# A decoder in two layers: VectorE takes a row's router logits ahead of the first maximum of an iteration of cross attention

## What is computed

```
x = x + L0_attn(layernorm(x));   x = x + L0_xattn(layernorm(x), ctx);   x = x + L0_ffn(layernorm(x))
x = x + L1_attn(layernorm(x));   x = x + L1_xattn(layernorm(x), ctx);   x = x + L1_ffn(layernorm(x))

xattn:  q, k, v in 16 heads of 16 channels;  scores = q k^T / 4;  softmax over 375 keys;  (attn v) Wo + bo
ffn:    logits = x Wr + br  (8 experts);  the best two (layer 0) or one (layer 1) of 8 experts per token
```

## Time and profile before

| | |
|---|---|
| median of the runs | 1463.95 us (1462.85 to 1476.16) |
| span of the profiled execution | 1473.2 us |
| iterations 3 to 13 of cross attention, layer 0 and layer 1, in that execution | 194.7 us each |
| TensorE busy, matmuls / weight loads | 89% / 70% of the span |
| VectorE, ScalarE, GpSimd busy | 48%, 38%, 30% |

### The profile page before, as it was taken

How to read it: one execution, slowest core, us unless ns; L and a number is a source line. 1 busy time by engine, 2 the same in 40 slices (tenths; PEclk the granted TensorE clock), 3 DMA queues, 4 the chain that set the end, 5 groups by cost and what they waited for, 6 DMA issues and landing times. The chain is left out here.

```text
span 1473.2 us, 34595 instructions
## 1 busy us (share of the span) xinstructions
PE 1305.0 (89%) x13568; PEld 1036.2 (70%) x13568; DVE 701.9 (48%) x1744; ACT 558.2 (38%) x1246; POOL 444.8 (30%) x654
## 2 busy tenths in 40 slices
PE   5998899999998389999994999799999998559996
PEld 2665457777776279999993777557777776459996
DVE  4885345555552612222222999545565552323322
ACT  2776035555554012222221555135555553112221
POOL 5994300000000155556552221200000000135662
PEclk8999579999998589999997999799999997569999
DMA  7000111111110369999984000011111110279994
GB/s 241 2 2 2 23 26 36 36 36 37 36 36 17 128 225 340 346 347 337 329 320 107 1 1 1 15 29 42 44 44 43 42 43 25 80 192 347 356 368 147
DMA packets 61355, 177.89 MB, mean 121 GB/s; under 512 B 20608, under 2 KB 41953, under 8 KB 46756
## 3 DMA queue, kind: packets, MB, share of 16 engines
q0 software_dynamic: 22176, 141.55, 27.0%
q1 hardware_dynamic: 39044, 34.46, 9.2%
HBM read 147.62 MB, written 12.85 MB: 109 GB/s over the span
## 5 line engine op out<-in xcount | busy, mean ns | idle before, releaser
L975 DVE TENSOR_REDUCE xa_mx<-xa_ps_s 112x2 f32<-112x750 f32 x246 | 231.5, 941 | 219.4 <-PE xa_ps_s L704 215.9
L892 ACT ACTIVATE xa_p<-xa_ps_p 125x672 f32<-125x672 f32 x256 | 187.2, 731 | 236.2 <-PE xa_ps_p L710 236.2
L710 PEld LDWEIGHTS xa_ps_p<-xa_qT,xa_kT 32*125 32x125 f32 x3072 | 199.4, 191 | 95.3 <-ACT xa_p L892 66.8
L710 PE MATMUL xa_ps_p<-xa_qT,xa_kT 32*125 32x112 f32 x3072 | 243.4, 291 | 24.4 <-DVE xa_mx L975 10.4
L704 PE MATMUL xa_ps_s<-xa_kT,xa_qT 32*112 32x375 f32 x984 | 224.8, 534 | 1.0 <-DMA xa_qT<-xa_qU 1.0
L1803 PEld LDWEIGHTS ex_ps_h<-ex_xT,ew_w 128*128 128x128 f32 x1792 | 213.7, 196 | 4.8 <-issue 2.0
L1803 PE MATMUL ex_ps_h<-ex_xT,ew_w 128*128 128x128 f32 x1792 | 214.3, 279 | 1.3 <-ACT ex_xT L1833 1.3
L1814 PE MATMUL ex_ps_y<-ew_w,ex_hT 128*128 128x256 f32 x896 | 202.7, 379 | 0.0
L1814 PEld LDWEIGHTS ex_ps_y<-ew_w,ex_hT 128*128 128x128 f32 x896 | 165.9, 190 | 20.2
L1837 ACT ACTIVATE ex_hT<-ex_ps_h,ew_w 128x128 f32<-128x128 f32 x224 | 70.1, 364 | 282.5 <-PE ex_ps_h L1803 282.5
L1849 DVE TENSOR_SCALAR ex_hT<-ex_ps_h,ew_w 128x128 f32<-128x128 f32 x224 | 68.2, 346 | 163.7 <-PE ex_ps_h L1803 163.7
(11 more groups left out here) (304 smaller groups left out, 2000.0 us busy)
## 6 DMA issues: line engine op xcount, KB each, us to landing
xa_kT<-xa_kU SPq DMA_DIRECT2D x128, 93.8 KB, 2.2
xa_qT<-xa_qU SPq DMA_DIRECT2D x64, 56.0 KB
xn<-xa_x SPq DMA_DIRECT2D x32, 112.0 KB, 2.2
lin_yg<-ys SPq DMA_DIRECT2D x16, 224.0 KB, 5.2
cT<-in_ctxT SPq DMA_DIRECT2D x4, 750.0 KB, 8.3
xa_qT<-xa_nmT SPq DMA_DIRECT2D x128, 1.8 KB
x<-in_x SPq DMA_DIRECT2D x4, 448.0 KB, 6.2
xn<-x SPq DMA_DIRECT2D x16, 112.0 KB, 2.1
```

Source lines behind the costliest of these rows:

```text
L710: return pe.matmul(bp[0:CT, i, c * S:(c + 1) * S], kT[r:r + 32, b % RB, n, c * CT:(c + 1) * CT], qT[r:r + 32, b % RB, n, :], start=True, s ...
L892: act.activation(p[slot % 4][:, :, :], bp[0:CT, :, 0:NC3 * S], ACT.Exp).then_inc(exped, 1)
L975: dve.tensor_reduce(mx[:, b % 2, j:j + 2, n], score_banks(b, pair)[0:S, :, 0:CL], AX, ALU.max).then_inc(maxed, 1)
```

## The change

At slot 0 of each iteration, VectorE's list has `row_logits(t-3)` ahead of `maximum`, and not behind it. Nothing else is edited.

```
             for t in range(-3, NB + 3):
                 for slot in range(8):
                     sb, sp = ahead(t, slot)
+                    if slot == 0 and on(t - 3):
+                        row_logits(t - 3)
                     if on(sb):
                         maximum(sb, sp)
-                    if slot == 0 and on(t - 3):
-                        row_logits(t - 3)
                     if slot == 0 and on(t - 2):
                         finish(t - 2)
```

## The result

The changed kernel takes 1453.32 us, the median of 20 runs (1442.10 to 1468.35), against 1462.59 us for the kernel before (20 runs, 1454.66 to 1481.75). The ratio is 0.9928, with a 95% interval from 0.9902 to 0.9953: 0.7% faster, 9.3 us by the medians; the interval is 7 to 14 us. Forecast were 1452.3 us and a gain of 11.7 us.

What follows compares the result with a forecast made beforehand. TensorE, busy for 89% of the span, was taken to bound the kernel. Ending 22 waits at 0.53 us each took 11.7 us off the runs' 1463.95 us, giving 1452.3 us, range 1448.0 to 1462.5 us.

Steps and rivals of the forecast that it cites:

- The wait and its size: Key products, iterations 3 to 13, both layers: they no longer wait for the maximum, 22 x 0.53 = 11.7 us gained.
- VectorE at no cost: Slot 0 on VectorE: row_logits ahead of the maximum delays nothing, costed at nothing.
- its fallback price: VectorE at slot 0, without idle time to hide the moved instruction: at most 0.156 us each, 22 x 0.156 = 3.4 us.
- a sign of being wrong: Prediction wrong if the maximum of round 0 starts later than 0.94 us behind round 0.
- the cover: VectorE's 1.41 us of idle time ahead of the maximum, of which the moved instruction needs 0.156 us.
- the rival's rule: Logits block VectorE: a late router product delays maximum and round 1, 22 us per us beyond 0.49 us; chance 0.01.
- What is late next: Round 1, at 2.37 us behind round 0: maximum, exponential and keys are ready 0.49, 0.60 and 0.9 us ahead.
- None takes the place of the wait: Ahead of round 1, neither maximum, exponential nor key transfers become a new wait.
- The rival that I gave 0.06: Keys land late and round 1 waits: 0.65 us per case, 1460 us if all took 3.3 us; chance 0.06.
- the likeliest case: Full gain in iterations 3 to 13 of both layers, by itself 1448.5 to 1455 us; chance 0.72.
- The span and the median: End of cross attention, layer 1: its 9.7 us clock loss explains the profiled span's 9.25 us above the median.
- The rivals on the clock: Clock falls at cross attention's end: one layer in the median run, 1462.0 us, chance 0.13; both layers, 1471.7 us, 0.04.

Runs made afterwards that it cites:

- the late product: The changed kernel with the router product moved behind the values of the next iteration: 1475.84 us, ratio 1.0031 to the kernel before.

## Why the prediction was right, and where its steps were not

**The wait and its size: right.** 0.53 us an iteration, in place of 0.50 by the idle time, held in 20 of the 22 iterations of the profile, and in all 22 once the keys come in time. Iteration 2 of layer 1 served as a run of the change in the trace before: same work, without the wait. The Trainium skill's sentence on weight loads pulled ahead ("TensorE: Matmul & The Clock Gate", on engine queues) bears on the 0.03 us between the two figures; the trace after agrees: the keys' weights load from 1007.95, while the values' matmuls run to 1008.02, behind 0.18 us of PEld idle time and not 0.72.

**VectorE at no cost: right, its fallback price untested.** The maximum starts 0.95 us behind round 0, a hundredth past the 0.94 that was named as a sign of being wrong, and nothing hangs on it. For the case that the cover were gone I put "at most 0.156 us for each". That can hold only where the product is there in time: in the late product the maximum is put back by 1.27 us, since it waits for as long as the instruction ahead of it does. The Trainium skill states VectorE's strict order ("TensorE: Matmul & The Clock Gate", on the array's architecture); the trace of that run agrees, with 2.29 us of idle time and the scores ready. What such a delay costs an iteration, by the rival's rule 22 us in all for each us beyond the slack of 0.49, stays open, because the keys' wait, and not the maximum, set round 1 there.

**What is late next: wrong in part.** "None takes the place of the wait" is refuted for the keys' transfers, in 2 of 22 iterations, by 1.00 and 0.73 us. The failed step took the longest landing in two stretches, 2.8 us, for a bound, and the landing of 3.3 us outside them for a stray. Of the 90 transfers there the trace has a landing for 68 only. Both readings belonged to one trace, in which no 16 KB of code start 1.2 to 1.4 us behind a key transfer of the stretches that has a landing on record. That the shorter iteration meets the fetching of code at other places is argued, not shown; with 2.37 us instead of 2.90 to round 1 less of a late landing stays hidden. The late iterations account for the difference between 11.7 us and the 9.7 us of the stretches. The rival that I gave 0.06 came true in small part, together with the likeliest case; I had priced one late landing at 0.65 us, and in the three traces they cost 0.73 to 1.18.

**The span and the median: a wrong reading, harmless.** I put the 9.25 us between them down to the end of cross attention in layer 1. The profile after has much the same losses there (50.7 and 56.1 us, 106.8 together, where 105.9 stood), with a span of 1446.2 us, below its median. The larger part of the 27 us between the spans lies ahead of all iterations that the change touches: iteration 3 of layer 0 starts at 235.2, not at 249.1. A stretch ahead of it shows why, kernel before and after:

```profile
141.00:200.00 59.00, 53.71 (x187) 0.51 0.08 18
...
141.00:200.00 59.00, 48.47 (x408) 0.86 0.11 25
```

The granted clock is 0.51 there in one execution and 0.86 in the other, and in the same 59 us 187 matmuls are done or 408. By their starts, 13.9 us of the 27.0 come from what lies ahead of iteration 3 of layer 0 and 10.3 from the stretches. Executions of one kernel differ by as much: in the three traces of the changed kernel this iteration starts at 235.2, 235.6 and 253.1 us, and the second of them takes 599.8 us from the end of the first stretch to the start of the next, where the others take 581.4 and 582.0. So a span, or a few runs, can't weigh a change of 10 us. The rivals on the clock were priced from the two layers of one execution; no run shows that price to be one of the change.

**Luck in the number.** The time came within 1.0 us of the forecast, but two misses cancel in part: 2.4 us of the gain by the medians are missing, and the median of three runs that the forecast started from lies 1.4 us above that of 20. The run times alone, with an interval of 7 to 14 us, can't tell 11.7 from 9.7; the stretches do.

## What to carry to other kernels

An instruction of 0.16 us that puts away a small result belongs ahead of the long one in the same list, if what it frees is waited for and what it waits for is over earlier by the order of the producing engine: its worth is the wait that it ends, 0.5 us an iteration here, and not its own length. Where a loop's first iterations lack one step, they are a free run of the kernel without that step's waits; reading a whole iteration there gives the gain more surely than adding idle times (0.53 us here, which is what came, and not 0.50). A shorter loop also uses up the slack that hid rare delays, so a transfer's slowest landing in one trace is no bound for the kernel after. And a time that comes out as expected isn't yet its cause: in the late product, only the row that directly precedes round 1 told which wait was paid.

## What the runs showed of the hardware

In the eight traces, 736 of 760 key transfers land 2.0 to 3.2 us behind their issue and 24 over 3.3 us, up to 4.2. For 22 of the 24 a transfer of program code of 16 KB starts 1.2 to 1.4 us behind the issue. The same two iterations are hit in all three traces of the changed kernel, and in one trace 32 products more ahead of the loop move the late landings to others. GpSimd issues such a transfer in 0.57 us, SyncE in 0.54 to 0.56, and it lands 2.4 us behind the issue, against 2.2.
